# Head attention on Trainium2: a block's output is copied to SBUF by ScalarE and turned there by VectorE in four pieces

## Chip, cores and metric

The kernel runs on 1 core of one Trainium2 chip. The metric is the device time of one execution in microseconds (us). The core has five engines with a queue each: TensorE (PE; its weight loads are listed as PEld), VectorE (DVE), ScalarE (ACT), GpSimd (POOL) and SyncE (SP, which issues transfers). They meet only through semaphores: an instruction may wait until a counter has reached a value, and may raise one when it is done.

## What is computed

One macaron block on x of shape (2, 2048, 256) in float32: half a feed-forward attention, a multi-head attention block, and half a feed-forward attention again.

```python
x = x + 0.5 * ffn_attention(layernorm(x), ...)    # tree-routed leaf MLPs give q, k, v; softmax attention
x = x + attention_block(layernorm(x), ...)        # the stage that is changed
x = x + 0.5 * ffn_attention(layernorm(x), ...)

# in attention_block: 16 heads of 16 columns, a reshape without a transpose, so that there are
# 32 blocks (batch x head) of 2048 rows by 16 columns
att = softmax(einsum('nqd,nkd->nqk', qm, km))
att_out = einsum('nqk,nkd->nqd', att + batch_pos, vm)   # batch_pos: a table by q - k, per head
```

## The kernel before

The program is a row of stages. The one that the change touches is `head_attend` (L1219), which takes 32 blocks (`BLOCKS`; n counts them), each in two halves (units, u = 2n and 2n + 1; the even half comes first). One half has 16 steps (c = 0 to 15).

**TensorE** runs `step(u)` (L1539). In every step it makes two `scan` products for a half that comes later (L1492, into the PSUM tile `s1_ps` of four banks), two `score` products (L1504, into `s2_ps`), and the `products` of probabilities and values of two steps ago (L1513, into `o_ps`). The scans run LEAD = 14 steps plus one half ahead, the products run LATE = 2 steps behind. In step c = 1 of the even half it also makes `positions` (L1519, instructions at L1529) for the next head, in blocks 0 to 29, right behind the last `products` of the block before; that last one raises `o_made`. In step c = 2 of the even half, `products` starts to overwrite `o_ps`, and so it waits at L1556.

**VectorE** takes the row maxima of each pair of scans: `scan_max` (L1581), one reduction of 1024 columns of PSUM a step. It frees the two banks (`s1_free`), for which `scan` waits, two pairs later. Behind the first four reductions of each half it does one small operation each for the half before (`max_parts`): negated maximum L1588, high part L1592, low part L1595, 32-column turn L1601. Behind the last reduction of an odd half (e = 30, which VectorE reaches when TensorE is at `positions`) stands `turn_out` (L1604): the block's output, 512 columns of `o_ps`, is turned in 32x32 squares into `oT` (L1609), then the row sums are inverted (L1612). `turn_step` counts both.

**ScalarE** takes the exponential of each score product (L1648, two a step), and in step c = 1 of the even half copies the positional products out of PSUM (`copy_positions`, L1637). It frees the score banks (`s2_free`).

**GpSimd** runs this loop over n: load the values of block n + 2 (L1391), place those of n + 1 (L1399), prepare the positional operands of a later head (`prepare_below` or `prepare_above`: one multiplication L1412, fifteen chained sums L1416, more behind them; while (n + 5) // 2 < 16, so in blocks up to 26), then `finish(n)`: wait for `turn_out`, normalise (L1444), add the positional part (L1450), store (L1452), and load the next block's positional part (L1395). So what GpSimd does after `finish(n)` starts when VectorE has inverted the row sums of block n.

**SyncE** issues loads of queries and keys, and eight small transfers for each half's maxima (L1335) when `mT_made` is raised.

Of the kernel before, what the change touches and what calls it, by code (L numbers as in the profile page):

```python
# [14 lines left out]
P = 128  # L15
# [13 lines left out]
HEADS, DH = 16, 16  # L29
BLOCKS = B * HEADS  # L30
RC = D // DH
# [918 lines left out]
def head_project(nc, tag, x_in, w, y_d, parts_d, v_d, table_d, skew_d, stacks, scan_loaded, ones_set, finished):  # L950

    with ExitStack() as ctx:
# [11 lines left out]
        BANKS = QK + 2  # L964
        TURN_AT = 2

# [93 lines left out]
        def _(dve):  # L1060
# [47 lines left out]
            for t in range(TILES):  # L1108
                if t + 2 < TILES:
                    moments(t + 2)  # L1110
                for n in range(QK):
                    if n == TURN_AT:
                        if t + 2 < TILES:
# [105 lines left out]
def head_attend(nc, tag, stacks, scan_loaded, ones_set, parts_d, v_d, table_d, skew_d, pos_d, att_d):  # L1219
# [3 lines left out]
    with ExitStack() as ctx:  # L1223
        def sb(name, shape, dt=F32):
            return ctx.enter_context(nc.sbuf_tensor(f"{name}_{tag}", shape, dt))
# [4 lines left out]
        def sem(name):  # L1230
            return ctx.enter_context(nc.semaphore(f"{name}_{tag}"))
# [8 lines left out]
        PAIR = 2  # L1240
# [3 lines left out]
        LEAD, LATE = 14, 2  # L1244
# [4 lines left out]
        POS_AT = LATE - 1  # L1249
# [8 lines left out]
        nmax = sb("nmax", [P, UC])  # L1258
        mparts = sb("mparts", [P, 2, PARTS, UC], F32R)
        mT = sb("mT", [P, 2, 2 * PARTS * UC])  # L1260
        oT = sb("oT", [P, RC, COLS])
        rinv = sb("rinv", [P, RC])
        onorm = sb("onorm", [P, D])
# [15 lines left out]
        o_ps = ps("o_ps", [P, 512])  # L1279
# [5 lines left out]
        s1_made, s1_free = sem("s1_made"), sem("s1_free")  # L1285
        s2_made, s2_free = sem("s2_made"), sem("s2_free")
        max_step, mT_made, m_loaded = sem("max_step"), sem("mT_made"), sem("m_loaded")
        o_made, turn_step, fin_step = sem("o_made"), sem("turn_step"), sem("fin_step")
        sum_step, pos_stored = sem("sum_step"), [sem("pos_stored0"), sem("pos_stored1")]
        stored = sem("att_stored")  # L1290
        LOADS = 2 * TERMS
        HEAD_LOADS = 3 + B
        MLOADS = QUADS * PARTS
        MSTEPS = 3
        FSTEPS = 2
        BELOW_STEPS, ABOVE_STEPS = RC + 4, RC + 5
        SUMS = BELOW_STEPS + ABOVE_STEPS
# [91 lines left out]
        def _(pool):  # L1389
# [49 lines left out]

            def finish(n):  # L1440
                k = n % 2
                pool.wait_ge(turn_step, 2 * n + 2)
                rs = rinv[:, :].rearrange("p (c o) -> p c o", o=1).broadcast_to([P, RC, DH])
                nc.gpsimd.tensor_tensor(onorm[:, :].rearrange("p (c d) -> p c d", d=DH), oT[:, :, 0:DH], rs,  # L1444
                                        ALU.mult).then_inc(fin_step, 1)
                pool.wait_ge(fin_step, FSTEPS * n + 1)
                pool.wait_ge(pos_loaded[k], 16 * (n // 2 + 1))
                if n > 0:
                    pool.wait_ge(stored, 16 * n)
                nc.gpsimd.tensor_tensor(att[:, :], onorm[:, :], posn[:, k, :], ALU.add).then_inc(fin_step, 1)  # L1450
                pool.wait_ge(fin_step, FSTEPS * (n + 1))
                pool.dma_start(rows(att_d, n), att[:, :]).then_inc(stored, 16)  # L1452
# [33 lines left out]
        def _(pe):  # L1486
# [52 lines left out]
            def step(u):  # L1539
                n = u // 2  # L1540
                if u % 2 == 0:
                    pe.wait_ge(score_loaded[n % SLOTS], 16 * LOADS * (n // SLOTS + 1))
                    pe.wait_ge(v_placed, n + 1)
                pe.wait_ge(m_loaded, 16 * MLOADS * (u + 1))
                for c in range(RC):
                    ahead = PAIR * (c + LEAD)
                    to, e = u + 1 + ahead // SCANS, ahead % SCANS
                    if to % 2 == 0 and e == 0 and to < UNITS:
                        pe.wait_ge(scan_loaded[to // 2 % SLOTS], 16 * LOADS * (to // 2 // SLOTS + 1))
                    for k in range(PAIR):  # L1550
                        if to < UNITS:
                            scan(to, e + k)
                        score(u, c, k)
                    if c >= LATE:
                        if c == LATE and u % 2 == 0 and n > 0:
                            pe.wait_ge(turn_step, 2 * n - 1)  # L1556
                        products(u, c - LATE)
                    elif u > 0:
                        products(u - 1, RC + c - LATE)
                    if c == POS_AT and u % 2 == 0 and n // 2 + 1 < HEADS:  # L1560
                        positions(n // 2 + 1, n % 2)
# [9 lines left out]
            for u in range(UNITS):  # L1571
                step(u)
# [3 lines left out]
        @block.vector  # L1576
        def _(dve):
            def scan_max(u, e):
                dve.wait_ge(s1_made, SCANS * u + e + 2)
                at = u % RING * SCANS + e  # L1580
                nc.vector.reduce_max(mx[:, at:at + 2], s1_ps[:, e % BANKS:e % BANKS + 2, :], AX_X).then_inc(s1_free, 1)  # L1581

            def max_parts(u, i):

                if i == 0:
                    dve.wait_ge(s1_free, SCANS // 2 * (u + 1))
                    at = u % RING * SCANS
                    nc.vector.reduce_max(nmax[:, :], mx[:, at:at + SCANS].rearrange("p (c g) -> p c g", g=QG),  # L1588
                                         AX_X, negate=True).then_inc(max_step, 1)
                elif i == 1:  # L1590
                    dve.wait_ge(max_step, MSTEPS * u + 2)
                    nc.vector.tensor_copy(mparts[:, 0, 0, :], nmax[:, :]).then_inc(max_step, 1)  # L1592
                elif i == 2:
                    dve.wait_ge(max_step, MSTEPS * u + 3)
                    nc.vector.tensor_tensor(mparts[:, 0, 1, :], nmax[:, :], mparts[:, 0, 0, :].bitcast(F32),  # L1595
                                            ALU.subtract).then_inc(max_step, 1)
                else:
                    dve.wait_ge(max_step, MSTEPS * (u + 1) + 1)
                    if u >= 2:
                        dve.wait_ge(m_loaded, 16 * MLOADS * (u - 1))  # L1600
                    nc.vector.transpose(mT[:, u % 2, :],  # L1601
                                        mparts[:, :, :, :].rearrange("p z a c -> p (z a c)").bitcast(F32)).then_inc(mT_made, 1)

            def turn_out(n, i):  # L1604
                if i == 0:
                    dve.wait_ge(o_made, n + 1)
                    if n > 0:
                        dve.wait_ge(fin_step, FSTEPS * n)
                    nc.vector.transpose(oT[:, :, :].rearrange("p c r -> p (c r)"), o_ps[:, :]).then_inc(turn_step, 1)  # L1609
                else:  # L1610
                    dve.wait_ge(turn_step, 2 * n + 1)
                    nc.vector.reciprocal(rinv[:, :], oT[:, :, DH]).then_inc(turn_step, 1)  # L1612

            TURN_AT = PAIR * (LEAD + LATE) - 2
            nc.vector.memset(mparts[:, 1].bitcast(F32), 0.0).then_inc(max_step, 1)
            for u in range(UNITS):
                for e in range(0, SCANS, 2):
                    scan_max(u, e)
                    if u > 0 and e // 2 <= MSTEPS:
                        max_parts(u - 1, e // 2)  # L1620
                    if u % 2 == 1 and u >= 3 and e == TURN_AT:
                        for i in range(2):
                            turn_out(u // 2 - 1, i)
            for i in range(MSTEPS + 1):
                max_parts(UNITS - 1, i)
            turn_out(BLOCKS - 1, 0)
            turn_out(BLOCKS - 1, 1)

        @block.scalar
        def _(act):  # L1630
            def copy_positions(h, half):
                turn = turn_of["pos", h, half]
                groups = slice(half * RC // 2, (half + 1) * RC // 2)
                act.wait_ge(s2_made, turn + 1)
                if h > 0:
                    act.wait_ge(pos_stored[(h - 1) % 2], 16 * 2 * B * ((h - 1) // 2 + 1))
                nc.scalar.copy(pos[:, half, groups, :].rearrange("p g w -> p (g w)"),  # L1637
                               s2_ps[:, turn % TURNS, 0:RC * W // 2]).then_inc(s2_free, 1)

            for half in range(2):  # L1640
                copy_positions(0, half)
            for u in range(UNITS):
                n = u // 2
                for i in range(UNIT):
                    c, g = i // PAIR, i % PAIR
                    turn = turn_of["score", u, i]
                    act.wait_ge(s2_made, turn + 1)
                    nc.scalar.activation(probs[:, (RC * u + c) % (LATE + 1), 4 * g:4 * g + 4, :].rearrange("p c t -> p (c t)"),  # L1648
                                         s2_ps[:, turn % TURNS, :], ACT.Exp).then_inc(s2_free, 1)
                    if c == POS_AT and g == PAIR - 1 and u % 2 == 0 and n // 2 + 1 < HEADS:  # L1650
                        copy_positions(n // 2 + 1, n % 2)


def head_close(nc, tag, w, att_d, y_d, x_in, x_out):
# [425 lines left out]
```

## Time and profile before

| | |
|---|---|
| median of 3 runs | 3017.08 us (3011.81 to 3024.38) |
| the profiled execution's own time | 3022.94 us |
| its span in the profile | 3021.1 us |
| PE, DVE, ACT, POOL busy over the span | 2805.2, 2143.6, 1800.7, 801.5 us |
| the changed stage in the profile | about 840 to 2187 us |
| DVE busy in 1300 to 1800 us | 490.93 of 500 us |
| PE busy in 1300 to 1800 us | 494.98 of 500 us |
| ACT busy in 1300 to 1800 us | 424.08 of 500 us |

How to read it: the profile gives each instruction with its source line, the tile that it writes and the tiles that it reads (out<-in), its start and its length. An engine's idle time is put down to the semaphore that came last. TensorE's busy time is modelled, since matmuls overlap. A timeline lists instructions in order of time and merges equal ones that follow each other (x12). Starts in a timeline are microseconds from the span's start.

### The profile page before, as it was taken

The page shows a single profiled execution, that of the slowest core. Times are in us where ns is not written, and L with a number is a line of the kernel's source. Part 1 is how long each engine was busy: PE and PEld are TensorE (multiplying, and loading weights), DVE is VectorE, ACT ScalarE, POOL GpSimd, SP SyncE. Part 2 cuts the span into 40 slices and gives each one's busy share as a digit, 9 for nine tenths or more (in the row PEclk, how much of TensorE's full clock was granted, in tenths as well). Part 3 has the DMA queues.
Part 4 walks back from the last instruction along what each step waited for, and adds up shares of the span by engine and source line. Part 5 has one row for each costly group of instructions (what it writes and reads, how often), then busy time and mean ns, then how long its engine had stood idle before and what let it go on. Part 6 is the DMA issues. An engine that isn't in the chain of part 4 may idle for free. (4 is left out here: it accounts for less than half of the span.)

```text
span 3021.1 us, 57357 instructions
## 1 busy us (share of the span) xinstructions
PE 2805.2 (93%) x21096; PEld 1725.5 (57%) x21096; DVE 2143.6 (71%) x3412; ACT 1800.7 (60%) x3507; POOL 801.5 (27%) x1290
## 2 busy tenths in 40 slices
PE   4998999998799999999999999999786699899999
PEld 2877888886543333333333333333253377788888
DVE  5545555445589999999999999999344555555554
ACT  3445343335268888888888888888633355443333
POOL 4652300002352233322333222300012564320000
PEclk8999999998789999999999999999997799999999
DMA  8994211106954454454555454442043699221100
GB/s 261 292 303 126 67 31 32 32 23 221 263 68 61 59 69 63 55 67 58 63 68 68 59 66 53 55 57 33 13 158 113 187 306 304 74 60 32 32 27 21
DMA packets 442366, 302.17 MB, mean 100 GB/s; under 512 B 167768, under 2 KB 418748, under 8 KB 442092
## 3 DMA queue, kind: packets, MB, share of 16 engines
q1 hardware_dynamic: 413292, 214.59, 34.9%
q0 software_dynamic: 28800, 83.92, 8.9%
q8 instruction: 173, 2.83, 0.4%
q14 instruction: 101, 0.83, 0.1%
HBM read 183.27 MB, written 118.78 MB: 100 GB/s over the span
## 5 line engine op out<-in xcount | busy, mean ns | idle before, releaser
L1581 DVE TENSOR_REDUCE mx_ha<-s_ps_ha 128x2 f32<-128x1024 f32 x1024 | 1237.8, 1219 | 32.0 <-PE s_ps_ha L1492 27.3
L1648 ACT ACTIVATE probs_ha<-s_ps_ha 128x512 f32<-128x512 f32 x2048 | 1111.7, 595 | 169.0 <-PE s_ps_ha L1504 25.1
L1492 PE MATMUL s_ps_ha<-ks_ha,qs_ha 48*128 48x512 f32 x2048 | 760.7, 452 | 23.9 <-DVE mx_ha L1581 14.2
L1504 PE MATMUL s_ps_ha<-qs_ha,ks_ha 50*128 50x512 f32 x2048 | 747.9, 445 | 0.0
L1513 PE MATMUL o_ps_ha<-probs_ha,vs_ha 128*32 128x256 f32 x8192 | 654.1, 391 | 1.4 <-DVE oT_ha L1609 1.4
L1492 PEld LDWEIGHTS s_ps_ha<-ks_ha,qs_ha 48*128 48x128 f32 x2048 | 308.4, 188 | 444.9 <-DVE mx_ha L1581 388.7
L908 ACT ACTIVATE probsT_a<-pT_ps_a 128x512 fp32r<-128x512 f32 x256 | 146.3, 597 | 422.6 <-PE pT_ps_a L778 422.6
L1513 PEld LDWEIGHTS o_ps_ha<-probs_ha,vs_ha 128*32 128x32 f32 x8192 | 161.2, 108 | 375.6 <-ACT probs_ha L1648 352.0
L1504 PEld LDWEIGHTS s_ps_ha<-qs_ha,ks_ha 50*128 50x128 f32 x2048 | 302.0, 185 | 12.4 <-ACT probs_ha L1648 11.9
L1444 POOL TENSOR_TENSOR onorm_ha<-oT_ha,rinv_ha 128x256 f32<-128x256 f32 x32 | 19.9, 623 | 929.8 <-DVE rinv_ha L1612 929.8
L821 DVE TENSOR_REDUCE nmax_a<-s_ps_a 128x1 f32<-128x2048 f32 x64 | 146.7, 2292 | 155.3 <-PE s_ps_a L767 155.3
L728 POOL DMA_INDIRECT rows_a<-ys_d,slots x96 | 90.7, 945 | 620.0 <-PE turn_ps_a L750 572.1
L449 DVE COPY y_p<-y_ps_p 128x256 f32<-128x256 f32 x282 | 119.5, 424 | 190.2 <-PE y_ps_p L591 152.1
L253 POOL DMA_INDIRECT xs_d<-xn_p,row_of_p x192 | 186.2, 970 | 165.9 <-PE xT_ps_p L555 68.9
L481 ACT ACTIVATE h_p<-h_ps_p,wa_p 65x128 f32<-65x128 f32 x282 | 102.3, 363 | 170.8 <-PE h_ps_p L581 166.9
L767 PE MATMUL s_ps_a<-k0T_a,qT_a 128*128 128x512 f32 x768 | 202.2, 408 | 0.0
L581 PE MATMUL h_ps_p<-xsT_p,wa_p 128*65 128x128 f32 x1128 | 175.3, 278 | 25.2 <-issue 19.9
L767 PE MATMUL s_ps_a<-k1T,qT_a 128*128 128x512 f32 x768 | 190.4, 398 | 0.0
L800 PE MATMUL o_ps_a<-v_a,probsT_a 128*128 128x512 f32 x512 | 188.8, 408 | 0.0
L800 PE MATMUL o_ps_a<-v,probsT_a 128*128 128x512 f32 x512 | 188.5, 408 | 0.0
L581 PEld LDWEIGHTS h_ps_p<-xsT_p,wa_p 128*65 128x65 f32 x1128 | 134.6, 139 | 70.7 <-issue 37.9
L591 PE MATMUL y_ps_p<-leaf_w_p,h_p 65*128 x564 | 171.7, 386 | 0.6 <-issue 0.5
(221 smaller groups left out, 3884.0 us busy)
## 6 DMA issues: line engine op xcount, KB each, us to landing
xs_p<-xs_d SPq DMA_DIRECT2D x282, 128.0 KB
ys_d<-y_p SPq DMA_DIRECT2D x66, 512.0 KB
qs_ha<-parts_d SPq DMA_DIRECT2D x192, 128.0 KB, 4.5
ks_ha<-parts_d SPq DMA_DIRECT2D x192, 128.0 KB, 5.1
parts_d<-parts_hp POOLq DMA_DIRECT2D x32, 512.0 KB, 7.6
qs_ha<-mT_ha SPq DMA_DIRECT2D x512, 1.0 KB
xs_d<-y_p SPq DMA_DIRECT2D x6, 1024.0 KB, 12.4
leaf_w_p<-in_wa SPq DMA_DIRECT2D x4, 1048.0 KB
```

Of the source, the lines that this page charges most:

```text
L253: pool.indirect_dma_start(xs_d[f], bass.IndirectOffsetOnAxis(row_of[:, f, t:t + 1], 0), xn[:, t, :], None).then_inc(scattered[f], 16)
L581: last = nc.tensor.matmul(h_ps[0:W1C, n % 2, 0:P], wa[:, n % WB, c * W1C:(c + 1) * W1C], xsT[:, n % 2, c, :], start=(c == 0), stop=(c == C ...
L591: nc.tensor.matmul(y_ps[:, n % 2, 0:D], h[:, n % 2], leaf_w[0:W1C, n // SEG % 2, bass.ds(at + LA, D)], start=True, stop=True).then_inc(y_m ...
L767: last = nc.tensor.matmul(s_ps[:, g, :], qT[:, i % 2, hq, c, :], kT[b][:, hk, c, g * 512:(g + 1) * 512], start=(c == 0 and n == 0), stop=( ...
L800: nc.tensor.matmul(o_ps[:, :], probsT[:, 0, g, k * P:(k + 1) * P], value.rearrange("p h d -> p (h d)"), start=first, stop=False)
L821: nc.vector.reduce_max(nmax[:, :], s_ps[:, :, :].rearrange("p a b -> p (a b)"), AX_X, negate=True).then_inc(max_done, 1)
L908: nc.scalar.activation(probsT[:, 0, g, :], pT_ps[:, g % 2, :], ACT.Identity).then_inc(pT_high, 1)
L1492: nc.tensor.matmul(s1_ps[:, e % BANKS, :], qs[0:QKROWS, k, c, :], ks[0:QKROWS, k, g * 4:(g + 1) * 4, :].rearrange("p c t -> p (c t)"), sta ...
L1504: nc.tensor.matmul(out, ks[LOW:LOW + KR, k, c, :], qs[LOW:LOW + KR, k, first:first + 4, :].rearrange("p c t -> p (c t)"), start=True, stop ...
L1513: last = nc.tensor.matmul(out, vs[:, u // 2 % SLOTS, c, :], probs[:, (RC * u + c) % (LATE + 1), :, i * COLS:(i + 1) * COLS], start=(c == 0 ...
L1581: nc.vector.reduce_max(mx[:, at:at + 2], s1_ps[:, e % BANKS:e % BANKS + 2, :], AX_X).then_inc(s1_free, 1)
L1648: nc.scalar.activation(probs[:, (RC * u + c) % (LATE + 1), 4 * g:4 * g + 4, :].rearrange("p c t -> p (c t)"), s2_ps[:, turn % TURNS, :], A ...
```

## The change

ScalarE copies a block's whole output from `o_ps` into a new SBUF tile `o_sb` in step c = 1 of the next block's even half, between its last exponential of that step and the copy of the positional products. TensorE now waits for this copy (`o_copied`) before it overwrites `o_ps`. VectorE's `turn_out` leaves its place at the end of the odd half; it is cut into four turns of 128 columns and the inversion, which stand behind the reductions e = 10, 14, 18, 22 and 26 of the even half that VectorE does next. For the last two blocks all five stand at the end. GpSimd's `finish` waits for the fifth.

```diff
+        o_sb = sb("o_sb", [P, 512])
...
+        PIECES = 4
+        TSTEPS = PIECES + 1
...
             def finish(n):
                 k = n % 2
-                pool.wait_ge(turn_step, 2 * n + 2)
+                pool.wait_ge(turn_step, TSTEPS * (n + 1))
...
                         if c == LATE and u % 2 == 0 and n > 0:
-                            pe.wait_ge(turn_step, 2 * n - 1)
+                            pe.wait_ge(o_copied, n)
...
             def turn_out(n, i):
                 if i == 0:
-                    dve.wait_ge(o_made, n + 1)
+                    dve.wait_ge(o_copied, n + 1)
                     if n > 0:
                         dve.wait_ge(fin_step, FSTEPS * n)
-                    nc.vector.transpose(oT[:, :, :].rearrange("p c r -> p (c r)"), o_ps[:, :]).then_inc(turn_step, 1)
+                if i < PIECES:
+                    groups, cols = slice(i * RC // PIECES, (i + 1) * RC // PIECES), slice(i * P, (i + 1) * P)
+                    nc.vector.transpose(oT[:, groups, :].rearrange("p c r -> p (c r)"), o_sb[:, cols]).then_inc(turn_step, 1)
                 else:
-                    dve.wait_ge(turn_step, 2 * n + 1)
+                    dve.wait_ge(turn_step, TSTEPS * n + PIECES)
                     nc.vector.reciprocal(rinv[:, :], oT[:, :, DH]).then_inc(turn_step, 1)
 
-            TURN_AT = PAIR * (LEAD + LATE) - 2
+            TURN_AT = {10: 0, 14: 1, 18: 2, 22: 3, 26: 4}
...
-                    if u % 2 == 1 and u >= 3 and e == TURN_AT:
-                        for i in range(2):
-                            turn_out(u // 2 - 1, i)
+                    if u % 2 == 0 and u >= 4 and e in TURN_AT:
+                        turn_out(u // 2 - 2, TURN_AT[e])
...
-            turn_out(BLOCKS - 1, 0)
-            turn_out(BLOCKS - 1, 1)
+            for n in range(BLOCKS - 2, BLOCKS):
+                for i in range(TSTEPS):
+                    turn_out(n, i)
...
+            def copy_out(n):
+                act.wait_ge(o_made, n + 1)
+                if n > 0:
+                    act.wait_ge(turn_step, TSTEPS * (n - 1) + PIECES)
+                nc.scalar.copy(o_sb[:, :], o_ps[:, :]).then_inc(o_copied, 1)
...
-                    if c == POS_AT and g == PAIR - 1 and u % 2 == 0 and n // 2 + 1 < HEADS:
-                        copy_positions(n // 2 + 1, n % 2)
+                    if c == POS_AT and g == PAIR - 1 and u % 2 == 0:
+                        if n > 0:
+                            copy_out(n - 1)
+                        if n // 2 + 1 < HEADS:
+                            copy_positions(n // 2 + 1, n % 2)
+            copy_out(BLOCKS - 1)
```

## Rows read from the trace of the kernel before

**Rows 1.** Groups by line, 800 to 2180 us: busy us, mean ns | idle, releasers

```profile
L1581 DVE TENSOR_REDUCE mx_ha<-s_ps_ha 128x2 f32<-128x1024 f32 x1024 | 1237.8, 1219 | 32.0 <-PE s_ps_ha L1492 27.3
L1492 PE MATMUL s_ps_ha<-ks_ha,qs_ha 48*128 48x512 f32 x2048 | 760.7, 452 | 23.9 <-DVE mx_ha L1581 14.2 <-PEq L952 9.7
...
L1513 PE MATMUL o_ps_ha<-probs_ha,vs_ha 128*32 128x256 f32 x8192 | 654.1, 391 | 1.4 <-DVE oT_ha L1609 1.4
```

**Rows 2.** Waits of PE, same stretch: us in total, times, longest

```profile
PE s_ps_ha L1492 <- DVE mx_ha L1581: 14.2, 39, 0.6
```

**Rows 3.** ACT timeline, four positional copies, then three late ones: start, us

```profile
1518.55 0.37 ACT L1637 COPY pos_ha<-s_ps_ha 128x256 f32<-128x256 f32 x1 [1.17 <-PE s_ps_ha L1529]
...
1642.74 0.37 ACT L1637 COPY pos_ha<-s_ps_ha 128x256 f32<-128x256 f32 x1 [1.16 <-PE s_ps_ha L1529]
...
1973.83 0.37 ACT L1637 COPY pos_ha<-s_ps_ha 128x256 f32<-128x256 f32 x1 [1.16 <-PE s_ps_ha L1529]
...
2055.69 0.37 ACT L1637 COPY pos_ha<-s_ps_ha 128x256 f32<-128x256 f32 x1 [1.16 <-PE s_ps_ha L1529]
```

**Rows 4.** DVE timeline from one block's end into the next even half

```profile
1512.80 4.92 DVE L1581 TENSOR_REDUCE mx_ha<-s_ps_ha 128x2 f32<-128x1024 f32 x4
1517.64 0.71 DVE L1609 STREAM_TRANSPOSE oT_ha<-o_ps_ha 128x512 f32<-128x512 f32 x1
1518.38 0.25 DVE L1612 RECIPROCAL rinv_ha<-oT_ha 128x16 f32<-128x16 f32 x1
1519.21 1.22 DVE L1581 TENSOR_REDUCE mx_ha<-s_ps_ha 128x2 f32<-128x1024 f32 x1 [0.57 <-PE s_ps_ha L1492]
...
1521.58 0.57 DVE L1592 CAST mparts_ha<-nmax_ha 128x8 fp32r<-128x8 f32 x1
1522.07 1.21 DVE L1581 TENSOR_REDUCE mx_ha<-s_ps_ha 128x2 f32<-128x1024 f32 x1
1523.20 0.68 DVE L1595 TENSOR_TENSOR mparts_ha<-nmax_ha,mparts_ha 128x8 fp32r<-128x8 f32 x1
1523.81 1.21 DVE L1581 TENSOR_REDUCE mx_ha<-s_ps_ha 128x2 f32<-128x1024 f32 x1
1524.94 0.20 DVE L1601 STREAM_TRANSPOSE mT_ha<-mparts_ha 128x32 f32<-128x32 f32 x1
```

**Rows 5.** DVE timeline, window 1526.1 to 1529: reductions behind schedule

```profile
1525.07 4.57 DVE L1581 TENSOR_REDUCE mx_ha<-s_ps_ha 128x2 f32<-128x1024 f32 x4
```

**Rows 6.** POOL timeline of the same block

```profile
1521.55 0.55 POOL L1391 DMA_DIRECT2D vflat_ha<-vh_d  x1
1522.11 0.74 POOL L1399 TENSOR_TENSOR vs_ha<-vflat_ha,unit_ha 128x256 f32<-128x256 f32 x1
1522.80 1.04 POOL L1412 TENSOR_TENSOR above_ha<-vp_ha,far_ha 128x512 f32<-128x512 f32 x1
1523.93 4.87 POOL L1416 TENSOR_TENSOR above_ha<-above_ha 128x32 f32<-128x32 f32 x15
...
1530.99 1.28 POOL L1405 TENSOR_TENSOR distantp_ha<-distant_ha,distantp_ha 128x512 fp32r<-128x512 f32 x1
```

**Rows 7.** PE timeline of the same block: the pause

```profile
1523.37 0.50 PE L1492 MATMUL s_ps_ha<-ks_ha,qs_ha 48*128 48x512 f32 x1
...
1525.07 0.49 PE L1492 MATMUL s_ps_ha<-ks_ha,qs_ha 48*128 48x512 f32 x1 [0.40 <-DVE mx_ha L1581]
```

**Rows 8.** DVE timeline of the same block's odd half

```profile
1540.61 1.22 DVE L1581 TENSOR_REDUCE mx_ha<-s_ps_ha 128x2 f32<-128x1024 f32 x1
1541.75 0.16 DVE L1592 CAST mparts_ha<-nmax_ha 128x8 fp32r<-128x8 f32 x1
1541.84 1.22 DVE L1581 TENSOR_REDUCE mx_ha<-s_ps_ha 128x2 f32<-128x1024 f32 x1
1542.99 0.16 DVE L1595 TENSOR_TENSOR mparts_ha<-nmax_ha,mparts_ha 128x8 fp32r<-128x8 f32 x1
```

**Rows 9.** DVE timeline of block 28, where POOL prepares nothing

```profile
2015.41 1.23 DVE L1581 TENSOR_REDUCE mx_ha<-s_ps_ha 128x2 f32<-128x1024 f32 x1 [0.57 <-PE s_ps_ha L1492]
...
2018.28 1.21 DVE L1581 TENSOR_REDUCE mx_ha<-s_ps_ha 128x2 f32<-128x1024 f32 x1
```

**Rows 10.** PE timelines at the start of blocks 30 and 31, and ACT's at block 30

```profile
2096.47 0.64 PE L1513 MATMUL o_ps_ha<-probs_ha,vs_ha 128*32 128x256 f32 x8 [0.70 <-DVE oT_ha L1609]
...
2136.71 0.64 PE L1513 MATMUL o_ps_ha<-probs_ha,vs_ha 128*32 128x256 f32 x8 [0.71 <-DVE oT_ha L1609]
...
2094.36 1.83 ACT L1648 ACTIVATE probs_ha<-s_ps_ha 128x512 f32<-128x512 f32 x3
```

**Rows 11.** DVE and POOL timelines at the stage's end

```profile
2174.00 0.72 DVE L1609 STREAM_TRANSPOSE oT_ha<-o_ps_ha 128x512 f32<-128x512 f32 x1 [36.06 <-PE o_ps_ha L1513]
2174.75 0.25 DVE L1612 RECIPROCAL rinv_ha<-oT_ha 128x16 f32<-128x16 f32 x1
...
2175.09 0.61 POOL L1444 TENSOR_TENSOR onorm_ha<-oT_ha,rinv_ha 128x256 f32<-128x256 f32 x1 [35.21 <-DVE rinv_ha L1612]
```

More of the change, by code:

```diff
@@ L1287, in head_attend @@
         max_step, mT_made, m_loaded = sem("max_step"), sem("mT_made"), sem("m_loaded")
-        o_made, turn_step, fin_step = sem("o_made"), sem("turn_step"), sem("fin_step")
+        o_made, o_copied, turn_step, fin_step = sem("o_made"), sem("o_copied"), sem("turn_step"), sem("fin_step")
         sum_step, pos_stored = sem("sum_step"), [sem("pos_stored0"), sem("pos_stored1")]
```

## The prediction, made before the changed kernel was built

> **What bounds the kernel now.** I read the groups by line first, then the waits, then the timelines of VectorE, GpSimd and TensorE over one block. In the changed stage TensorE waits for little: 14.2 us in 39 pauses for VectorE's maxima, 1.4 us for the turned output [rows 1, 2]. So it sets the pace. Four reductions at that pace take 4.92 us, the last one being 1.22 long, which makes (4.92 - 1.22) / 3 = 1.23 us a step [rows 4]. When VectorE is behind, four take 4.57 us with a last one of 1.21: (4.57 - 1.21) / 3 = 1.12 us, say 1.13 [rows 5]. VectorE alone thus needs 1.13, and wins back 0.10 us on TensorE in every step in which it does nothing else.
>
> The positional copies give the length of a block: (1642.74 - 1518.55) / 3 = 41.40 us in the middle, (2055.69 - 1973.83) / 2 = 40.93 us late [rows 3]. So a block in which GpSimd prepares operands loses 0.46 us; there are 26 of those (blocks 1 to 26). Where it goes is seen in one block. VectorE begins the even half at 1519.21, and would begin its next reductions 1.2335 apart (40.93 less 1.46 for the positional products, over 32). Its high part (L1592) takes 0.57 us in place of 0.16, its low part (L1595) 0.68 in place of 0.16 [rows 4, 8]. Both end within 0.05 us of a GpSimd instruction: the load's issue that ends at 1522.10, the multiplication that ends at 1523.84 [rows 6]. The reduction at 1523.81 is then 1523.81 - (1519.21 + 3 x 1.2335) = 0.90 us late, and TensorE, which needs the banks that it frees, starts a scan at 1525.07 in place of 1523.37 + 1.23 = 1524.60, so 0.46 late [rows 7]. VectorE may therefore be 0.90 - 0.46 = 0.44 us late at no cost. A block without preparation bears this out: there only the high part is held, the reduction at 2018.28 is 2018.28 - (2015.41 + 2.47) = 0.40 late [rows 9], and the block still takes 40.93.
>
> **The turn's old place** costs nothing in these blocks: the turn and the inversion end at 1518.63, and VectorE still idles 0.57 us until TensorE is back from the positional products [rows 4]. Taking it away gains nothing there.
>
> **The copy.** 30 of 32 new copies of 512 columns stand beside positional products. I price one at an exponential of the same shape, 0.60 us: 1.83 us for three, the first two 0.49 apart in start [rows 10]; the nearest copy, of 256 columns, took 0.37, so 0.37 to 0.74. ScalarE idles 1.17 us there [rows 3], so it costs nothing; without that cover it would hold up the exponentials by 0.5. Queued behind it are the positional copy and the next exponentials; the wait for `o_made` is over before, since those products come ahead of the positional ones. TensorE's new wait ends earlier than the old one.
>
> **The pieces.** The turn of 32 columns from SBUF takes 0.20 us, that of 512 from PSUM 0.71 [rows 4]; in between, 128 columns give 0.20 + 96 x 0.51 / 480 = 0.30 us. What such an operation takes from the pace is less than its length: from 1523.81 the next reduction starts 1.26 later, 0.13 over 1.13, for a length of 0.20 [rows 4, 5]. So a piece costs 0.23 and the inversion (0.25) 0.18. Bounds: 0.13 (the 32-column turn) to 0.64 (the whole turn); I take 0.23 since its row is the same operation with SBUF as source. From e = 10 to e = 30 there are eleven steps that win back 11 x 0.10 = 1.14 (at 0.1035), against 4 x 0.23 + 0.18 = 1.10. VectorE is at most 4 x 0.23 - 7 x 0.1035 = 0.20, or with the first steps' rounding 0.25, late: under 0.44, so TensorE doesn't pause, and the odd half begins about on time.
>
> **GpSimd moves by 18 us.** This is what I expect to change the time. `finish` waits for the inversion, and the operations behind it keep their distances: the multiplication starts 1522.80 - 1518.38 = 4.42 us after the inversion starts [rows 4, 6]. Let 0 be the start of the even half on VectorE. The inversion now starts at 13 x 1.2335 + 0.14 (lateness) + 1.14 (a reduction's start to the next operation) = 17.3. GpSimd is busy until 1532.3 - 1518.4 = 13.9 later, to 31; the even half's small operations, at 1 to 6, meet nothing and cost what they do in the quiet half [rows 8]. The 0.46 goes. But the odd half's now meet it: the high part comes at 17 x 1.2335 + 0.02 + 1.14 = 22.13, the multiplication runs from 21.73 to 22.78. The high part waits for its end, and the next reduction starts 0.03 before that end (1523.81 against 1523.84): at 22.75, that is 0.55 late. The low part, 1.13 later, meets the sums (0.25 long, every 0.33; 15 in 4.87 us [rows 6]) and waits up to 0.25: lateness about 0.63. TensorE pauses 0.63 - 0.44 = 0.19, say 0.20. Each block gains 0.46 - 0.20 = 0.26; times 26 = 6.8 us.
>
> **The ends.** Blocks 30 and 31 have no positional products; there TensorE waited 0.70 and 0.71 us for the turn [rows 10], which ended at 2096.42. The copy would follow the second exponential, at 2094.36 + 2 x 0.50 = 2095.36 to 2095.45, and end by 2096.04, about 0.4 sooner: 0.8 us gained for both. At the end of the stage the turn of 0.72 us gives way to a copy (0.60), one hop between engines (0.08, from the inversion's end at 2175.00 to GpSimd's start at 2175.09 [rows 11]) and four pieces (0.30 + 3 x 0.23 = 0.99): 0.95 us added. Net + 0.1 us.
>
> **Sum.** -6.8 + 0.1 = -6.7 us. The profiled execution took 3022.94 us (span 3021.1 and 1.8 around it), so 3016.2; it lies 5.9 above the median of the runs, 3017.08, so the forecast of a median is 3010.4 us.
>
> **Rivals.**
> - *The pause vanishes altogether.* If the multiplication ends 0.2 us sooner against the high part, or starts 0.4 later, the lateness stays under 0.44. Then 26 x 0.46 = 12.0 us go: 3005.2. For it: the collision rests on a 0.4 us margin. Against: the distances repeat to a few hundredths. Chance 0.20.
> - *The worst meeting.* Everything 0.35 later, and the high part waits for the whole multiplication: lateness 0.55 + 0.35 + 0.10 = 1.0, pause 0.57, 26 x 0.11 = + 2.9 us: 3020. Chance 0.13.
> - *Dear pieces: slower.* The mechanism is VectorE's reserve in the even half. Behind the old turn the inversion starts 0.03 after it ended, 1518.38 against 1518.35 [rows 4], so without overlap. If a piece costs its length and such gaps, 0.34, then 4 x 0.34 - 7 x 0.1035 = 0.64 is over 0.44 and TensorE pauses 0.20 in the even half, 0.04 at the inversion, and the odd half begins 0.27 late and pauses 0.47: 0.71 a block, 26 x (0.71 - 0.46) = + 6.5 us: 3023.6. It decides from a piece of 0.30 on; slower by 15 us takes 0.42 a piece, and at the bound of 0.64 it would be + 35 us, 3052. Against it is the 32-column turn, which the reductions overlap. Chance 0.12. The Trainium skill speaks for this rival ("VectorE: DVE Perf Modes", "The DRAIN you can't avoid": the next op waits until the pipe has emptied, and op count is to be kept down); here the reduction behind the small turn started before that turn's record ended (1525.07 against 1525.14), which is the case that the page's own exception for ops that are not held allows.
> - *It doesn't do what it says.* If the small operations are slow for another reason than GpSimd's place, the even half keeps its 0.46, and the time stays: 3017. The meeting ends make this unlikely: 0.08.
>
> **How the numbers follow.** Forecast 0.47 (3010.4), the others as given. The range leaves out most of the dear case's upper end, and adds to 3005 and 3020 some 2 us for the scatter of medians (the runs spread from 3011.8 to 3024.4): 3003 to 3022. 0.5% is 15 us, about what can be told from no change here. A gain of 15 has no source in this trace, since all pauses that can go sum to 12.0 + 0.8: 0.05 for scatter and what I don't see. A loss of 15 needs pieces of 0.42: 0.04. Within: 0.91.
>
> **What would show it.** In the timeline of the changed kernel: L1592 and L1595 at 0.16 us in the even half, the high part near 0.65 in the odd half; TensorE's pauses for VectorE moved from the fourth step of the even to that of the odd half, near 0.2 each; a block of 41.1 us; pieces of 0.30; no wait of TensorE for the copy in the middle blocks. Wrong would be a piece over 0.35, pauses in the even half from e = 10 on, or a block at 40.93 or over 41.4.

## The result: 0.5% faster, TensorE's pauses in the blocks gone but for one of 0.07 us

The changed kernel took 3000.93 us (median of 5 runs, 2999.93 to 3010.37) against 3017.08 us before: a ratio of 0.9949, with a 95% interval from 0.9931 to 0.9967. By the ratio that is 15 us faster, between 10 and 21; the medians differ by 16. The prediction was 3010.4 us in a range from 3003 to 3022; the time lies 2 us under the range. The profiled execution's span is 3002.5 us against 3021.1.

From block 1 on, the profile after lists no wait of TensorE for VectorE's maxima any more, where before there was one in each of 26 blocks. (The 14.2 us of [rows 2] are counted from 800 us on and take in the waits ahead of that; such waits are there after the change too, 4.1 us in 14.) What is left for the output is the wait for ScalarE's copy in the two blocks that have no positional products. First the kernel before from 887 us on, then the changed one from 880:

```profile
PE s_ps_ha L1492 <- DVE mx_ha L1581: 10.7, 26, 0.6
...
PE o_ps_ha L1516 <- ACT o_sb_ha L1649: 0.4, 2, 0.2
```

Groups by line of the changed stage (busy us, mean ns | idle before them, releasers), the same lines as [rows 1] and the new ones:

```profile
L1584 DVE TENSOR_REDUCE mx_ha<-s_ps_ha 128x2 f32<-128x1024 f32 x1024 | 1224.2, 1212 | 57.2 <-PE s_ps_ha L1495 54.5
...
L1516 PE MATMUL o_ps_ha<-probs_ha,vs_ha 128*32 128x256 f32 x8192 | 654.3, 391 | 0.4 <-ACT o_sb_ha L1649 0.4
...
L1614 DVE STREAM_TRANSPOSE oT_ha<-o_sb_ha 128x128 f32<-128x128 f32 x128 | 37.8, 299 | 36.2 <-ACT o_sb_ha L1649 36.2
...
L1649 ACT COPY o_sb_ha<-o_ps_ha 128x512 f32<-128x512 f32 x32 | 19.0, 592 | 0.8 <-PE o_ps_ha L1516 0.8
```

VectorE's timeline over one block's even half and the start of its odd half (start, us), which answers to [rows 4 and 8]:

```profile
1506.52 1.23 DVE L1584 TENSOR_REDUCE mx_ha<-s_ps_ha 128x2 f32<-128x1024 f32 x1 [1.49 <-PE s_ps_ha L1495]
...
1508.89 0.16 DVE L1595 CAST mparts_ha<-nmax_ha 128x8 fp32r<-128x8 f32 x1
...
1510.12 0.16 DVE L1598 TENSOR_TENSOR mparts_ha<-nmax_ha,mparts_ha 128x8 fp32r<-128x8 f32 x1
...
1513.82 0.30 DVE L1614 STREAM_TRANSPOSE oT_ha<-o_sb_ha 128x128 f32<-128x128 f32 x1
1514.05 2.33 DVE L1584 TENSOR_REDUCE mx_ha<-s_ps_ha 128x2 f32<-128x1024 f32 x2
1516.29 0.30 DVE L1614 STREAM_TRANSPOSE oT_ha<-o_sb_ha 128x128 f32<-128x128 f32 x1
1516.51 2.33 DVE L1584 TENSOR_REDUCE mx_ha<-s_ps_ha 128x2 f32<-128x1024 f32 x2
...
1523.69 0.25 DVE L1617 RECIPROCAL rinv_ha<-oT_ha 128x16 f32<-128x16 f32 x1
...
1527.48 1.23 DVE L1584 TENSOR_REDUCE mx_ha<-s_ps_ha 128x2 f32<-128x1024 f32 x1
1528.62 0.56 DVE L1595 CAST mparts_ha<-nmax_ha 128x8 fp32r<-128x8 f32 x1
1529.09 1.21 DVE L1584 TENSOR_REDUCE mx_ha<-s_ps_ha 128x2 f32<-128x1024 f32 x1
1530.23 0.15 DVE L1598 TENSOR_TENSOR mparts_ha<-nmax_ha,mparts_ha 128x8 fp32r<-128x8 f32 x1
```

And GpSimd's in the same stretch, to be held against [rows 6]:

```profile
1527.40 0.74 POOL L1402 TENSOR_TENSOR vs_ha<-vflat_ha,unit_ha 128x256 f32<-128x256 f32 x1
1528.08 1.06 POOL L1415 TENSOR_TENSOR above_ha<-vp_ha,far_ha 128x512 f32<-128x512 f32 x1
1529.22 4.91 POOL L1419 TENSOR_TENSOR above_ha<-above_ha 128x32 f32<-128x32 f32 x15
```

The reader is to see three things. The even half's high and low parts (L1595, L1598) are back to 0.16 us each. The odd half's high part is held 0.56 us, until the multiplication ends at 1529.14; the reduction behind it is (1529.09 - 1527.48) - 1.23 = 0.38 us late. The low part slips in between two sums and isn't held here. That is not so every time: in the second profile of the changed kernel it took 0.25 us in 10 of the 26 blocks, and the reduction behind it came 0.45 late; these blocks took 40.93 to 40.95 us. And one block of the first profile, block 14, took 41.00: its high part took 0.70 us, and the reductions ran up to 0.52 late. ScalarE's two copies, start and length, in two blocks that follow each other:

```profile
1504.58 0.59 ACT L1649 COPY o_sb_ha<-o_ps_ha 128x512 f32<-128x512 f32 x1
1505.86 0.37 ACT L1642 COPY pos_ha<-s_ps_ha 128x256 f32<-128x256 f32 x1 [0.69 <-PE s_ps_ha L1532]
1545.52 0.59 ACT L1649 COPY o_sb_ha<-o_ps_ha 128x512 f32<-128x512 f32 x1
1546.80 0.37 ACT L1642 COPY pos_ha<-s_ps_ha 128x256 f32<-128x256 f32 x1 [0.68 <-PE s_ps_ha L1532]
...
1587.72 0.37 ACT L1642 COPY pos_ha<-s_ps_ha 128x256 f32<-128x256 f32 x1 [0.69 <-PE s_ps_ha L1532]
```

The copy fits in ScalarE's idle time (0.69 us of 1.17 are left), and a block takes (1587.72 - 1505.86) / 2 = 40.93 us in place of 41.40.

**What of the 15 us the two traces account for.** From the first positional products of block 1 to those of block 29, 28 blocks take 1158.1 us before and 1146.1 after: -12.0. Block 0 is 1.4 longer (42.19, 43.59), the end of TensorE's work is 1.0 nearer to the last positional products (119.83, 118.82), and the next stage begins 0.6 later behind it (20.65, 21.26). That is -11.0 us, inside the measured interval (from -10 to -21) at its edge. 7.3 us of the difference between the two spans lie ahead of the stage, where the programs are the same.

### The profile page after: what moved, and what is told of

It reads as the page before. It is cut to its first block and busy times, and to the rows that moved or that the text cites. A ratio compares the mean times of both kernels' runs of the same rounds, so it can differ in the third digit from the quotient of the medians.

```text
span 3002.5 us, 57516 instructions
## 1 busy us (share of the span) xinstructions
PE 2799.7 (93%) x21096; PEld 1721.2 (57%) x21096; DVE 2108.0 (70%) x3508; ACT 1816.9 (61%) x3539; POOL 802.5 (27%) x1290
## 5 line engine op out<-in xcount | busy, mean ns | idle before, releaser
L1584 DVE TENSOR_REDUCE mx_ha<-s_ps_ha 128x2 f32<-128x1024 f32 x1024 | 1224.2, 1212 | 57.2 <-PE s_ps_ha L1495 54.5
```

## The experiments

Theory A: TensorE is paced by itself as long as a reduction is no more than 0.44 us late; VectorE is late because two of its small operations are held by GpSimd's work, and the change gains because it puts that work elsewhere. Rival B: it gains by the turn's leaving VectorE's queue, or the output's leaving PSUM. Rival C: something outside the stage gains as well. The runs below were made on two chips on which the kernel before has medians of 3065 to 3070 us, each beside runs of it on the same chip.

**Only GpSimd's work moved**, the turn, the inversion and the copying left as before:

```diff
             def finish(n):
                 k = n % 2
                 pool.wait_ge(turn_step, 2 * n + 2)
+                if n + 2 < BLOCKS:
+                    pool.wait_ge(s1_free, SCANS // 2 * (2 * n + 4) + 14)
```

> The kernel before with one wait added and nothing else: GpSimd's finish(n) also waits for the 14th reduction of the even half after next (e = 26), the place where the changed kernel inverts. Turn, inversion and ScalarE stay as before. Theory A (the gain is GpSimd's work leaving the small operations of the even half): the blocks 1 to 26 take 40.93 us in place of 41.39, L1592 and L1595 take 0.16 us in the even half, sum of the blocks -12 us, whole kernel about 3005 to 3006. Rival B (the gain is the turn leaving VectorE's queue at the positional products, or TensorE's shorter wait for the output): nothing of it is in this kernel, 3017.

Measured: 3052.48 us against 3068.29, ratio 0.9932 (0.9907 to 0.9957). Blocks of 40.93 us without exception. VectorE's timeline at the start of an even half, with the turn in its old place, and of the next odd half:

```profile
1576.85 0.71 DVE L1611 STREAM_TRANSPOSE oT_ha<-o_ps_ha 128x512 f32<-128x512 f32 x1
1577.59 0.25 DVE L1614 RECIPROCAL rinv_ha<-oT_ha 128x16 f32<-128x16 f32 x1
1578.41 1.22 DVE L1583 TENSOR_REDUCE mx_ha<-s_ps_ha 128x2 f32<-128x1024 f32 x1 [0.57 <-PE s_ps_ha L1494]
...
1580.79 0.16 DVE L1594 CAST mparts_ha<-nmax_ha 128x8 fp32r<-128x8 f32 x1
...
1582.02 0.16 DVE L1597 TENSOR_TENSOR mparts_ha<-nmax_ha,mparts_ha 128x8 fp32r<-128x8 f32 x1
...
1600.50 0.47 DVE L1594 CAST mparts_ha<-nmax_ha 128x8 fp32r<-128x8 f32 x1
```

One wait on an engine that is busy a quarter of the time gives the whole gain. The turn's place and the copy are not needed for it: rival B falls as the main cause. The time is a little lower than the stage's 12 us account for. Timed again:

> The kernel before with GpSimd's one wait (14 reductions into the even half after next), timed again beside the run above. Theory A: blocks at 40.93 us and a ratio that the stage's -12 us gives, 0.996; the first time it was 0.993, lower than the stage accounts for. If 0.993 again, something outside the blocks gains; if 0.996, that was the scatter.

Measured: 3054.86 against 3070.47 us, ratio 0.9975 (0.9949 to 1.0); blocks of 40.93. The two ratios lie on either side of the 0.996 that the stage gives, but they don't say that the first was scatter: this one counts three executions of 12 that took 3079 to 3085 us. By medians the kernel was 15.8 us faster the first time and 15.6 now, both times some 4 more than the stage's 12.

**Only VectorE's small operations moved**, GpSimd left alone, in the kernel before:

```diff
+            PARTS_AT = {0: 0, 8: 1, 10: 2, 12: 3}
...
-                    if u > 0 and e // 2 <= MSTEPS:
-                        max_parts(u - 1, e // 2)
+                    if u > 0 and e in PARTS_AT:
+                        max_parts(u - 1, PARTS_AT[e])
```

> The kernel before with VectorE's small operations moved and GpSimd left alone: the high part, the low part and the small turn stand behind the reductions e = 8, 10 and 12 of each half in place of 2, 4 and 6 (the maximum stays at 0). In the even half they then meet GpSimd's chained sums (0.25 us each with gaps) and not the placing and the multiplication (0.74 and 1.05). Theory A: each is held 0.25 at most, lateness under 0.44, block 40.93 us, some -12 us, ratio 0.996. If GpSimd's work as such cost VectorE time wherever they overlap, or if the gain came of anything in the changed kernel but the meeting: 41.39 us.

Measured: 3053.45 against 3070.47 us, ratio 0.9948 (0.9933 to 0.9964). Blocks of 40.93 but for two (41.20 and 41.13); in the first of them TensorE waits 0.19 us for a transfer of the half's maxima, which this edit issues three steps later. The even half, while GpSimd adds up from 1530.21 to 1535.12 (VectorE's timeline, one line of GpSimd's behind it):

```profile
1531.56 0.25 DVE L1592 CAST mparts_ha<-nmax_ha 128x8 fp32r<-128x8 f32 x1
1531.73 1.21 DVE L1581 TENSOR_REDUCE mx_ha<-s_ps_ha 128x2 f32<-128x1024 f32 x1
1532.86 0.15 DVE L1595 TENSOR_TENSOR mparts_ha<-nmax_ha,mparts_ha 128x8 fp32r<-128x8 f32 x1
...
1530.21 4.91 POOL L1416 TENSOR_TENSOR above_ha<-above_ha 128x32 f32<-128x32 f32 x15
```

The same gain from the other side of the meeting, with GpSimd's work in its old place. So it is the meeting that costs, and which of GpSimd's operations is met: short ones with gaps cost 0.1 us, the long ones half a microsecond each.

**The inversion one step later**, in the changed kernel:

```diff
-            TURN_AT = {10: 0, 14: 1, 18: 2, 22: 3, 26: 4}
+            TURN_AT = {10: 0, 14: 1, 18: 2, 22: 3, 28: 4}
```

> The changed kernel with the inversion one step later (e = 28 in place of 26), so that GpSimd's work moves by 1.23 us against VectorE's small operations of the odd half. Theory A: the multiplication L1415 now runs from 22.8 to 23.86 after the even half's start and holds the low part (about 23.3) for 0.5; the high part (22.10) comes as the values are placed (22.12 to 22.86) and is either first or held 0.7. Lateness 0.45 to 0.6 or more, pause 0 to 0.2 a block, so 0 to 5 us over the changed kernel. Rival B: no difference.

Measured: 3086.81 against 3068.29 us, ratio 1.0047 (1.0022 to 1.0071): slower than before. Blocks of 42.10 us. VectorE's timeline at the odd half's high part, and GpSimd's:

```profile
1571.64 1.23 DVE L1584 TENSOR_REDUCE mx_ha<-s_ps_ha 128x2 f32<-128x1024 f32 x1
1572.78 1.81 DVE L1595 CAST mparts_ha<-nmax_ha 128x8 fp32r<-128x8 f32 x1
1574.50 1.21 DVE L1584 TENSOR_REDUCE mx_ha<-s_ps_ha 128x2 f32<-128x1024 f32 x1
...
1572.80 0.75 POOL L1402 TENSOR_TENSOR vs_ha<-vflat_ha,unit_ha 128x256 f32<-128x256 f32 x1
1573.49 1.06 POOL L1415 TENSOR_TENSOR above_ha<-vp_ha,far_ha 128x512 f32<-128x512 f32 x1
```

The direction was right and the size far off: I had let the high part in between the placing and the multiplication. It isn't let in. The multiplication starts at 1573.49 while the placing's record runs to 1573.55, and an operation on 8 columns waits 1.81 us for both. The reduction is (1574.50 - 1571.64) - 1.23 = 1.63 late, and the block is 1.17 longer.

**The copy alone**, in the kernel before: ScalarE copies as in the changed kernel, VectorE turns the copy whole in the old place.

```diff
-                            pe.wait_ge(turn_step, 2 * n - 1)
+                            pe.wait_ge(o_copied, n)
...
-                    dve.wait_ge(o_made, n + 1)
+                    dve.wait_ge(o_copied, n + 1)
...
-                    nc.vector.transpose(oT[:, :, :].rearrange("p c r -> p (c r)"), o_ps[:, :]).then_inc(turn_step, 1)
+                    nc.vector.transpose(oT[:, :, :].rearrange("p c r -> p (c r)"), o_sb[:, :]).then_inc(turn_step, 1)
```

> The kernel before with ScalarE's copy alone: the output is copied to SBUF beside the positional products, and VectorE turns the copy whole, in the old place at the end of the odd half. Theory A: the copy is hidden and gains nothing, blocks stay at 41.39 us; the turn starts some 0.3 us later and still ends before TensorE's next scans are there (0.57 us were idle), whole kernel 3016 to 3018. Rival B in its second form (TensorE's or VectorE's access to the PSUM tile was what cost): a gain of several us.

Measured: 3075.73 against 3068.29 us, ratio 1.0011 (0.9987 to 1.0034), no measurable change; but blocks of 41.66 us, 0.27 longer than before. The medians differ by 7.4 us, and from block 1 to block 29 the trace is 7.2 longer. In VectorE's timeline the engine idles 0.17 us for the copy, and the turn starts 1.31 us ahead of the even half's first reduction in place of 1.57 [rows 4], so 0.26 later; GpSimd's work moves with it, and now the low part falls across two of its operations:

```profile
1537.49 0.71 DVE L1610 STREAM_TRANSPOSE oT_ha<-o_sb_ha 128x512 f32<-128x512 f32 x1 [0.17 <-ACT o_sb_ha L1645]
...
1538.80 1.23 DVE L1582 TENSOR_REDUCE mx_ha<-s_ps_ha 128x2 f32<-128x1024 f32 x1 [0.31 <-PE s_ps_ha L1493]
...
1541.27 1.23 DVE L1582 TENSOR_REDUCE mx_ha<-s_ps_ha 128x2 f32<-128x1024 f32 x1
1542.41 1.34 DVE L1596 TENSOR_TENSOR mparts_ha<-nmax_ha,mparts_ha 128x8 fp32r<-128x8 f32 x1
1543.67 1.21 DVE L1582 TENSOR_REDUCE mx_ha<-s_ps_ha 128x2 f32<-128x1024 f32 x1
```

My "nothing" for the copy by itself was thus wrong in the trace: hidden on ScalarE, it moves GpSimd. The reduction behind the low part is 1543.67 - (1538.80 + 3 x 1.2335) = 1.17 late, and the block pays 0.73. The copy and the turn's source (0.71 us from SBUF as from PSUM) gain nothing: rival B falls in this form too.

**GpSimd's work wholly out of the way**: the wait of the first experiment, at the fifth reduction of the odd half.

```diff
+                if n + 2 < BLOCKS:
+                    pool.wait_ge(s1_free, SCANS // 2 * (2 * n + 5) + 5)
```

> The kernel before with one wait added: GpSimd's finish(n) waits until the fifth reduction of the odd half (21 reductions on from the even half's start), behind all small operations of VectorE, so that its work of 14 us meets none. Theory A: L1592 and L1595 take 0.16 us in both halves, and the block still takes 40.93 us as in the run with the wait at 14: a lateness under 0.44 us is free. Ratio as there within 0.002. Rival (every held operation costs, and the first wait left 0.3 us a block): 26 x 0.3 = 8 us faster than that run.

Measured: 3055.62 against 3064.93 us, ratio 0.9993 (0.9968 to 1.0018). In the profile no small operation is held (0.16 us in both halves), and the blocks take 40.93, as in the kernels that hold the high part for half a microsecond. So a lateness under the bound is free. The ratio doesn't follow the blocks, since 5 of 12 executions took 3077 to 3090 us (the others 3047 to 3056). The profiled one is of those, and shows where: TensorE's granted clock fell to half in the last block, in which there are no scans left. Stretches of the stage's end (busy us of PE, PEld, DVE, ACT, POOL, granted clock, DMA):

```profile
2110.00:2140.00 30.00, 29.30 (x288) 10.67 (x286) 29.84 (x35) 25.68 (x49) 1.34 (x2) 1.00 0.01 1
...
2170.00:2216.00 46.00, 46.00 (x225) 14.99 (x224) 0.00 (x0) 22.66 (x42) 0.00 (x0) 0.50 0.00 1
```

**The turn in one piece** at e = 10, in the changed kernel (the piece's columns follow from PIECES):

```diff
-        PIECES = 4
+        PIECES = 1
...
-            TURN_AT = {10: 0, 14: 1, 18: 2, 22: 3, 26: 4}
+            TURN_AT = {10: 0, 26: 1}
```

> The changed kernel with the turn whole, 512 columns from the copy at e = 10 (inversion still at 26). By the lateness rule: the next reduction starts 1.14 + 0.70 - 0.07 = 1.77 us after the last, 0.53 late, 0.09 over the 0.44 that is free; block 41.02 us, 3 us over the changed kernel. If cutting the turn was what gained: 41.4 us a block. If lateness were free up to two banks' worth (1.2 us): 40.93.

Measured: 3055.72 against 3064.93 us, ratio 0.9969 (0.9954 to 0.9985). Blocks of 41.00 us. VectorE's timeline:

```profile
1574.86 2.42 DVE L1584 TENSOR_REDUCE mx_ha<-s_ps_ha 128x2 f32<-128x1024 f32 x2
1577.20 0.70 DVE L1614 STREAM_TRANSPOSE oT_ha<-o_sb_ha 128x512 f32<-128x512 f32 x1
1577.82 9.40 DVE L1584 TENSOR_REDUCE mx_ha<-s_ps_ha 128x2 f32<-128x1024 f32 x8
```

The second of the two reductions started at 1574.86 + 2.42 - 1.22 = 1576.06, the next one at 1577.82: 1.76 apart, 0.53 late, pause 0.07. The cut into four is worth that much, 2 us in all, and not the gain.

**Every piece made twice**, the rival in which pieces are dear:

```diff
+                    nc.vector.transpose(oT2[:, groups, :].rearrange("p c r -> p (c r)"), o_sb[:, cols])
                     nc.vector.transpose(oT[:, groups, :].rearrange("p c r -> p (c r)"), o_sb[:, cols]).then_inc(turn_step, 1)
```

> The changed kernel with each piece made twice (the second copy of the turn is thrown away into a tile of its own), so each place costs VectorE about 0.52 us in place of 0.23. It is the rival of the prediction in which pieces are dear. By the lateness rule: 0.36 late behind the first, 0.60, 0.68 and 0.69 behind the others, pauses of 0.16 and about 0.24 and 0.24 in the even half; the inversion 0.33 later, so the high part of the odd half is held to 0.7 late, pause 0.3; together 0.9 a block, 41.8 us, some 26 us over the changed kernel. If VectorE had the reserve that its idle time suggests: 40.93.

Measured: 3073.80 against 3064.93 us, ratio 1.0028 (1.0014 to 1.0042). Blocks of 41.59 us, 0.66 over 40.93, where I had expected 0.9. Two pieces and the two reductions around them:

```profile
1594.19 0.27 DVE L1616 STREAM_TRANSPOSE oT_ha<-o_sb_ha 128x128 f32<-128x128 f32 x1
1594.38 2.32 DVE L1585 TENSOR_REDUCE mx_ha<-s_ps_ha 128x2 f32<-128x1024 f32 x2
...
1597.03 2.32 DVE L1585 TENSOR_REDUCE mx_ha<-s_ps_ha 128x2 f32<-128x1024 f32 x2
```

VectorE has no idle time left there, and each pair of steps takes it 1597.03 - 1594.38 = 2.65 us and not 2.47. By the 19th reduction, which starts at 1607.31, it is 1607.31 - (1584.02 + 18 x 1.2335) = 1.09 late, 1584.02 being the first, and the block loses 0.66. So the rival's mechanism is real, and it would have made the change slower than the kernel before; only its price doesn't hold for single pieces.

**No change**, the kernel before run as if it were one, and **the changed kernel again**:

> The kernel before, word for word, as if it were a change: what the comparison makes of no change, and whether block 0 and the time ahead of the stage scatter by themselves. Theory A: ratio 1.000 within 0.002, blocks 1 to 26 at 41.39 us, the stage's block 0 anywhere from 42 to 55 us by when TensorE's granted clock rises. Rival C (the changed kernels have a second gain ahead of the stage): block 0 and the stage's start always late here.

> The changed kernel as it is, timed again, to see how much of the 16 us is the stage and how much is the scatter of runs. The pieces of the stage that the two profiles show sum to -11 us (blocks -12.0, block 0 +1.4, the last two blocks -1.0, the end +0.6); 7 us more lay before the stage begins, where the programs are the same. Theory A: -11 to -12 us, ratio 0.996 to 0.9965. Rival C (there is a second effect outside the stage): -16 again, ratio 0.995, with the stage beginning some 7 us sooner again.

Measured: no change gives 3067.18 against 3064.93 us, ratio 1.0022 (1.0002 to 1.0042); the interval just misses one, so such a comparison is good to about 0.2% beyond its interval. The changed kernel gives 3058.42 against 3068.29 us, ratio 0.9954 (0.9933 to 0.9974). Rival C says that the programs also differ ahead of the stage. The profiles show no sign of it: block 0 begins at 871.6 us with the kernel before, at 870.2 with the changed one, and between 865.9 and 873.7 in the eight others. The medians of five comparisons with blocks of 40.93 us (the changed kernel twice, the first wait twice, the small operations later) are lower by 16, 10, 16, 16 and 17 us, where the stage accounts for 11 to 12. Four of the five thus lie 4 to 6 us beyond the stage and one 1 to 2 short of it. No change at all moved a median by 2 us, the other way; what the four have beyond the stage is more than that, and it stays open.

## Why the prediction was wrong, step by step

**The bound** held in every kernel. What a block loses is the lateness of its latest reduction less 0.43 to 0.46:

| kernel | latest reduction, us late | block, us | over 40.93 |
|---|---|---|---|
| before | 0.90 | 41.39 | 0.46 |
| before, block 14 | 1.06 | 41.54 | 0.61 |
| changed | 0.38 | 40.93 | 0 |
| changed, block 14 | 0.52 | 41.00 | 0.07 |
| the copy alone | 1.17 | 41.66 | 0.73 |
| inversion at 28 | 1.63 | 42.10 | 1.17 |
| one piece | 0.53 | 41.00 | 0.07 |
| pieces twice | 1.09 | 41.59 | 0.66 |

**The old place of the turn is worth nothing, the gain comes from GpSimd's move**: right, shown from both sides (the wait alone, the small operations alone).

**The even half is freed, the odd half is met**: right. The high part was forecast at about 0.65 us and took 0.56; the low part was to be held up to 0.25 and took 0.15, or 0.25 in 10 blocks of the second profile.

**The failed step is the lateness with which I placed the inversion**, the "0.14" in 13 x 1.2335 + 0.14 + 1.14 = 17.3 us. I let VectorE win back 0.10 us in each step behind a piece. But the step right behind a piece takes 2.33 - 1.22 = 1.11 us and not 1.13; a piece and its free step make 1516.51 - 1514.05 = 2.46 us, two steps of TensorE's pace, and nothing adds up. The inversion started 1523.69 - 1506.52 = 17.17 us into the half, the multiplication ended at 1529.14 - 1506.52 = 22.62 and not 22.78, and the reduction was 0.38 late in place of 0.55: on the other side of 0.44. The forecast then added 0.08 for the low part, to 0.63. In the profile of the result nothing was added; where the low part was held in the second profile, the reduction came 0.45 late, just at the bound, and the blocks lost 0.02 at most. So the 0.14 is what failed, and the pause of 0.20 us a block became nothing, which was the rival to which I gave a chance of 0.20. A block at 40.93 was also among the prediction's own signs of being wrong. That rival's sum, -12.0 us in the blocks, is what the trace shows. An error of 0.16 us decided over 5 us, and I should have seen that the forecast hung on a margin this thin, and given this case and the forecast about even chances.

**The ends**: the two waits went from 0.70 and 0.71 to 0.22 each (forecast: 0.4 gained each, came: 0.5). The last turn as four pieces took 0.89 us (forecast 0.99), and the way to the next stage grew by 0.6 (forecast 0.95).

**Prices**: the copy 0.59 us (forecast 0.60), a piece 0.30 (0.30), the inversion 0.25.

**The range** ended at 3003, since I took 2 us for the scatter of a median; that was too little. The kernel run against itself differs by 2.3 us in median, and single executions by 15 and more. Of the 9.5 us between forecast and time, 5.2 are the pause that didn't come (26 x 0.20); the better ends (-0.4 in place of +0.1) and the longer block 0 (+1.4) together take 0.9 back, and some 5 us are the part that stays open.

**The meetings were mis-sized in principle**: I took an operation of VectorE to be served between any two of GpSimd's. The high part of [rows 4] was let in behind a load's issue, but the trace before did hold a case against it, in block 14:

```profile
1439.87 1.23 DVE L1595 TENSOR_TENSOR mparts_ha<-nmax_ha,mparts_ha 128x8 fp32r<-128x8 f32 x1
...
1439.32 0.75 POOL L1399 TENSOR_TENSOR vs_ha<-vflat_ha,unit_ha 128x256 f32<-128x256 f32 x1
1440.01 1.05 POOL L1412 TENSOR_TENSOR above_ha<-vp_ha,far_ha 128x512 f32<-128x512 f32 x1
```

The low part asks as the values are placed and is not let in before the multiplication; it takes 1.23 us, and this block is the longest of the 26, 41.54. A reading of the longest and not only of the usual operation would have shown it. In the run with the later inversion, the error was 1.0 us a block. The worst meeting that I gave as a rival (pause 0.57) was too mild by half.

## What to carry to other kernels

When the pacing engine waits for buffers that another frees, work out how late the other may be before a pause begins, and read each change as a shift of lateness against that bound; under it, held or slow operations are free, over it each microsecond is paid in full (here the bound is 0.43 to 0.46 us). An operation that releases another engine's work moves that work in time, and with it all the meetings of two engines at a shared resource: look at what a moved release will run beside before looking at what its own engine saves. And when the forecast depends on a margin of a tenth or two of a microsecond, try the cheap experiment that moves only the release (here one wait), since it shows the whole effect without the rewrite.

## What the runs showed of the hardware

**VectorE's two-source and converting operations are held by GpSimd's operations, and not let in between two that follow without a gap.** The conversion of 8 columns takes 0.16 us alone, 0.56 behind the rest of one multiplication, 1.81 behind a placing and a multiplication. The low part's operation, also of 8 columns, took 1.34 across the same two in the run with the copy alone, and 1.23 in block 14 of the kernel before. The issue of a load by GpSimd (0.55 us) holds the conversion too, for 0.57 [rows 4 and 6]. The chained sums, which wait for each other and leave some 0.08 us, let both in (0.25 and 0.15 us). Neither the reductions nor the 32-column turn were ever held (in blocks 1 to 26 of all profiles 1.16 to 1.23 and 0.19 to 0.20 us). The Trainium skill ("SBUF — State Buffer", "Who interferes with whom") has the pair of ports that VectorE shares with GpSimd as an exclusive lock for the whole instruction; `cast` can take it, and an operation with two inputs in SBUF contends with a GpSimd operation that reads SBUF. The traces agree (0.56 and 1.34 in place of 0.16 us), and add the case without a gap.

**TensorE's granted clock makes block 0 longer by 11 us in one of two executions of the same program.** It stands at half (1.2 of 2.4 GHz) as the stage begins and rises within block 0. Thirty microseconds in block 0 of the two profiles of the changed kernel (PE, PEld, DVE, ACT, POOL, then the mean granted clock), where the block took 43.6 and 55.0 us:

```profile
846.00:876.00 30.00, 29.38 (x259) 12.30 (x257) 27.24 (x29) 23.56 (x44) 18.14 (x45) 0.92 0.53 73
```

```profile
870.00:900.00 30.00, 30.00 (x165) 11.37 (x167) 17.41 (x18) 14.74 (x28) 17.74 (x44) 0.50 0.53 65
```

Ahead of it TensorE had waited between stages. The second such place is the last block, where there are no scans left: in the profile of the run with GpSimd wholly out of the way the clock fell there, for 26 us more. Executions of such length came in 5 of 12 there and in 3 of 12 in the second run with one wait, but in none of the 57 of the kernels with ScalarE's copy, in which TensorE's pause at the start of that block is 0.22 and not 0.71 us. The pause alone can't decide it: the kernel before has the same 0.71 [rows 10], and executions 17 to 29 us above its median, at a mean granted clock of 0.95 as in those, came in 2 of 12 of its runs as no change and in 2 of 32 of those beside the first experiments, but in none of the 52 others; the first run with one wait had none in 9. What decides it was not tried.
